# A graph layer's second stage, regrouped: attribute turns once in eight rows, accumulator banks cleared by ScalarE, two rows mixed in one product, one-hots built per row

## The reference

```
h   = segment_sum(x[dst] * weight, src) @ W.T            # layer 1
x1  = layernorm(x + h)
# layer 2: tensor product of the 9 edge attributes with the source node
msg = sum_m attr[e, m] * (x1[src[e]] @ M_m)              # M_m: 128 x 128, built from w0..w4
y   = segment_sum(msg, dst)
out = layernorm(x1 + y)
```

## Time and profile before

| | |
|---|---|
| time, median of 3 runs | 4115.09 us (4114.18 to 4115.81) |
| the profiled execution's own time: its span | 5011.3 us |
| instructions recorded | 63448 |
| first gather of the second layer | at 1859.7 us |
| last gather of the second layer | at 4968.6 us |

### The profile page before, as it was taken

One profiled execution on the slowest core, in us unless ns is written; L12 is line 12 of the kernel. 1 busy time (PEld: TensorE's weight loads), 2 busy tenths in 40 slices (PEclk: granted clock), 3 DMA queues, 4 the chain that ended last, 5 costly groups with the idle time before them and its releaser, 6 DMA issues.

```text
span 5011.3 us, 63448 instructions
## 1 busy us (share of the span) xinstructions
PE 3029.2 (60%) x18004; PEld 2599.8 (52%) x18006; DVE 2089.5 (42%) x4613; ACT 1176.6 (23%) x2104; POOL 2759.7 (55%) x2887
## 2 busy tenths in 40 slices
PE   2100788888888864555555555555556555555666
PEld 1000778788887863444444444444445444444555
DVE  8999565565565661222222222222222222222333
ACT  5443444444444440000000000000000000000111
POOL 4000555555555536666666666666666666666664
PEclk6555899999999976777777777777777777777666
DMA  1001222222222231111111111111111111111221
GB/s 49 5 11 41 75 71 75 71 71 76 72 71 71 71 96 47 46 47 46 46 46 46 46 47 46 46 46 46 46 47 47 46 47 45 46 46 55 66 66 46
DMA packets 117978, 267.07 MB, mean 53 GB/s; under 512 B 52225, under 2 KB 52369, under 8 KB 116769
## 3 DMA queue, kind: packets, MB, share of 16 engines
q0 software_dynamic: 92080, 191.02, 13.1%
q1 hardware_dynamic: 21234, 66.99, 3.9%
q10 hardware_dynamic: 4608, 8.39, 0.4%
HBM read 251.19 MB, written 8.72 MB: 52 GB/s over the span
## 4 chain that ended last, share of the span: by engine, by line
another core or an unknown queue 34%; PE 11%; issue 10%; DVE 6%; DVEq 2%; ACT 0%; ACTq 0%
PE quad L1673 5%; PE mixed L1688 4%; DVE group L1784 3%; DVE hot L1758 1%; PE quad L1666 1%; PE attr_t L1639 1%; DVE acc L1790 1%; DVEq L1769 1%; DVE attr_hot L1763 0%; DVEq L1784 0%; DVEq L1758 0%; DVEq L1777 0%; DVEq L1780 0%; DVEq L1761 0%
## 5 line engine op out<-in xcount | busy, mean ns | idle before, releaser
L1558 POOL DMA_INDIRECT feat<-x,ids x2048 | 1940.6, 948 | 1181.8 <-issue 615.8
L1784 DVE TENSOR_TENSOR group<-group,quad 128x504 f32 (+1 forms) x512 | 347.3, 678 | 2301.9 <-remote 2167.5
L1134 POOL DMA_INDIRECT l_feat<-in_x,id_of x768 | 737.4, 960 | 916.5 <-ACT w_of L827 368.7
L1673 PE MATMUL quad<-attr_hot,feat 128*128 128x144 f32 x4096 | 842.8, 338 | 547.7 <-issue 544.3
L1673 PEld LDWEIGHTS quad<-attr_hot,feat 128*128 128x128 f32 x4096 | 661.0, 219 | 737.5 <-issue 736.4
L1688 PE MATMUL mixed<-group,mix 128*128 128x192 f32 x2304 | 691.1, 486 | 577.9 <-DVE group L1784 577.9
L1688 PEld LDWEIGHTS mixed<-group,mix 128*128 128x128 f32 x2304 | 650.5, 305 | 622.7 <-issue 556.8
L1599 ACT CAST ids<-src_col 128x8 int32 (+1 forms) x256 | 50.3, 197 | 2746.0 <-remote 2525.4
L1208 PE MATMUL got<-x_near,far_w 128*128 128x128 bf16 x4224 | 341.0, 220 | 160.3 <-issue 148.6
L1208 PEld LDWEIGHTS got<-x_near,far_w 128*128 128x128 bf16 x4224 | 278.7, 98 | 206.4 <-issue 192.1
L1036 DVE TENSOR_SCALAR keys<-swap,src_of,w_of 128x184 f32<-128x184 f32 x1024 | 308.2, 373 | 127.9 <-PE l_pre L1227 122.0
(11 more groups left out here) (249 smaller groups left out, 2929.8 us busy)
## 6 DMA issues: line engine op xcount, KB each, us to landing
place<-table SPq DMA_DIRECT2D x64, 640.0 KB
feat<-x,ids POOLq DMA_INDIRECT x2048
l_feat<-in_x,id_of POOLq DMA_INDIRECT x768
attr_in<-in_edge_attr SPq DMA_DIRECT2D x129, 72.0 KB
norm_x<-in_x SPq DMA_DIRECT2D x16, 256.0 KB, 2.7
x<-norm_z ACTq DMA_DIRECT2D x16, 256.0 KB, 2.4
x_t<-x SPq DMA_DIRECT2D x15, 256.0 KB
out<-z_t ACTq DMA_DIRECT2D x15, 256.0 KB
```

Of the source, the lines that this page charges most:

```text
L1134: pool.indirect_dma_start(feat[:, landing, :], None, x, bass.IndirectOffsetOnAxis(ap=id_of[s % 2][:, c:c + 1], axis=0)).then_inc(feat_in[l ...
L1558: pool.indirect_dma_start(feat[z][:, t, :], None, x1, bass.IndirectOffsetOnAxis(ap=ids[z][h][:, t % H:t % H + 1], axis=0),).then_inc(feat_ ...
L1673: last = nc.tensor.matmul(bank[:, :, bass.ds(places[t % H], WIN)], feat[z][:, t, :], attr_hot[h][:, t % H, :, :], start=False, stop=(t % Q ...
L1784: nc.vector.tensor_tensor(to, to, quad[:, q, 0:NA * QUAD_WIN].rearrange("p (m n) -> p m n", m=NA), ALU.add).then_inc(quad_added, 1)
```

## The change

The second layer is regrouped around steps of eight rows (an octet):

- attributes of eight rows are loaded at once (576 KB, 128 partitions) and turned by nine 128x128 transposes, in two parts, in the third and fifth row of each octet; ScalarE copies them from `attr_t` into the SBUF tile `attr_e`, from which VectorE reads;
- ScalarE clears the banks of `quad`, two at a time, after VectorE has added them; the matmuls by zeros go;
- two rows share one `group` tile and are mixed by one set of nine matmuls of 384 columns, one row later; VectorE adds both halves after that;
- `hot` and `attr_hot` are made once for each row, two rows ahead; `ids` once for four rows;
- POOL's loop has eight rows; its gathers and their waits on `half_summed` stay; they count on one semaphore per half row instead of one per quad.

```diff
-        ids = [[sb(f"ids{z}_{h}", [P, H], I32) for h in range(2)] for z in range(ROW_SLOTS)]
-        attr_in = [sb(f"attr_in{z}", [R, P * NA], F32) for z in range(2)]
-        hot = sb("hot", [P, H, WIN], F32)
-        attr_hot = [sb(f"attr_hot{h}", [P, H, NA, WIN], F32) for h in range(2)]
-        group = [sb(f"group{z}", [P, NA, GROUP_WIN], F32) for z in range(2)]
+        ids = [sb(f"ids{b}", [P, O // 2 * R], I32) for b in range(2)]
+        attr_in = sb("attr_in", [O * R, P * NA], F32)
+        attr_e = sb("attr_e", [P, NA, O * R], F32)
+        hot = sb("hot", [P, R, WIN], F32)
+        attr_hot = [sb(f"attr_hot{z}", [P, R, NA, WIN], F32) for z in range(2)]
+        group = [sb(f"group{z}", [P, NA, 2, GROUP_WIN], F32) for z in range(2)]
...
# GpSimd
+                with pool.Fori(0, OCTETS) as o:
+                    for j in range(O):
+                        z = j % S
+                        if j % (O // 2) == 0:
+                            pool.wait_ge(ids_made, w * (2 * OCTETS) + o * 2 + (j // (O // 2) + 1))
                         for h in range(2):
-                            pool.wait_ge(ids_made, w * (RN * 2) + i * (2 * ROW_SLOTS) + (z * 2 + h + 1))
+                            pool.wait_ge(half_summed, summed(w, o * O, (j - S) * 2 + h))
                             pool.sem_inc(g.turn, 1)
...
# ScalarE
+                def row(o, j, first=False, e=None):
+                    r = o * O + j
+                    u = w * RN + r
+                    if j % 2 == 1 and not (first and j == 1):
+                        act.wait_ge(pair_mixed, w * PAIRS + o * (O // 2) + (j - 3) // 2 + 1)
+                        clear_group((j - 3) // 2)
+                    act.wait_ge(quad_added, u * 4 + 2)
+                    clear_half(0)
+                    if e is not None:
+                        normalize(w, e)
+                    act.wait_ge(quad_added, u * 4 + 4)
+                    clear_half(1)
+                    if j % (O // 2) == O // 2 - 1:
+                        act.wait_ge(half_summed, summed(w, r, 1))
+                        copy_ids(...)
+                    if j == TURN_ROW - 1:
+                        copy_last()
+                    if j == TURN_ROW + 1:
+                        copy_attr(w * OCTETS + o + 1)
...
# TensorE
+                pe.wait_ge(quad_zero, u * 2 + (h + 1))
+                if h == 0:
+                    pe.wait_ge(hot_made, u + 2)
+                pe.wait_ge(feat_in[z % S][h], n_fill * (16 * H) + 16 * H)
+                for t in range(h * H, h * H + H):
+                    (the matmul of L1673, attr_hot[z % 2][:, t, :, :])
...
+                def row(o, j, first=False):
+                    for h in range(2):
+                        half_row(w, r, h, j, n_fill)
+                    if j % 2 == 0 and not (first and j == 0):
+                        mix(w * PAIRS + o * (O // 2) + (j - 2) // 2, (j - 2) // 2 % 2)
+                    turn_next(w * OCTETS + o + 1, j)
...
# VectorE
-                by_tile = attr_t[:, z, 0:NA * R].rearrange("p (m t) -> p t m", m=NA)
-                nc.vector.tensor_tensor(attr_hot[h][:], hot[:].unsqueeze(2).to_broadcast(s4),
-                                        by_tile[:, h * H:h * H + H, :].unsqueeze(3).to_broadcast(s4),
-                                        ALU.mult).then_inc(hot_made, 1)
+                by_tile = attr_e[:, :, j * R:(j + 1) * R].rearrange("p m t -> p t m")
+                nc.vector.tensor_tensor(attr_hot[z][:], hot[:].unsqueeze(2).to_broadcast(s4),
+                                        by_tile.unsqueeze(3).to_broadcast(s4), ALU.mult).then_inc(hot_made, 1)
...
+                    add_quads(w, r, n, j // 2 % 2, j % 2, 0, offs)
+                    if starts:
+                        add_pair(n - 1, starts)
+                    add_quads(w, r, n, j // 2 % 2, j % 2, 1, offs)
+                    next_hots(o, j)
```

More of the change, by code:

```diff
@@ L1543, in _ @@
             n_loads = sp.value_load(g.n_pass[0:1, 1:2], min_val=1, max_val=g.PASSES1)
-            for z in range(2):
-                sp.wait_ge(attr_here[z], n_loads * (8 * RN) + 16 * (1 - z))
+            sp.wait_ge(attr_here, n_loads * (16 * OCTETS) + 32)
             sp.sem_inc(loads_ended, 1)
@@ L1588, in _ @@
                 act.sem_inc(stored[s], 16)
[L1589 to L1592, removed]
-            with passes(act) as w:
[L1594 to L1606, removed]
+            for b in range(2):
+                copy_ids(b, b * (O // 2 * R))
@@ new lines, in mix @@
+            def mix(n, side):
+                pe.wait_ge(quad_added, n * 8 + 8)
+                pe.wait_ge(acc_added, n * 2 + 2)
+                pe.sem_inc(g.turn, 1)
+                to = mixed[:, 0:2 * GROUP_WIN].rearrange("p (a n) -> p a n", a=2)
+                for m in range(NA):
+                    last = nc.tensor.matmul(to, g.mix[:, m, :], group[side][:, m, :, :], start=(m == 0),
+                                            stop=(m == NA - 1))
+                last.then_inc(pair_mixed, 1)
@@ new lines, in turn_nodes @@
+            def turn_nodes(w, u, e):
+                pe.wait_ge(acc_added, u + 2 - e % 2)
+                pe.wait_ge(x_used, w * NE + e + 2)
+                pe.sem_inc(g.turn, 1)
+                for a in range(BATCH):
+                    last = nc.tensor.transpose(y[:, a * P:(a + 1) * P], nodes_of(e)[:, a, :],
+                                               g.cst[:, C_IDENT:C_IDENT + P])
+                last.then_inc(y_made, 1)
+            pe.wait_ge(attr_here, 16)
+            turn_attr((NA - 1,))
@@ L1658, in _ @@
+            pe.wait_ge(attr_out, 1)
+            turn_attr(range(NA - 1))
+            pe.wait_ge(tables_made, 1)
             with passes(pe) as w:
-                def row(r, half_r, z, v_half, e=None):
-                    u = w * RN + r
-                    turn_attr(u + 1, v_half, 1 - z)
+                def row(o, j, first=False):
+                    r = o * O + j
+                    n_fill = o * (O // S) + j // S
                     for h in range(2):
[L1663 to L1676, removed]
-                        if h == 0 and e is not None:
-                            pe.wait_ge(acc_added, u + 2)
-                            pe.wait_ge(x_used, w * NE + e + 2)
-                            pe.sem_inc(g.turn, 1)
-                            for a in range(BATCH):
-                                last = nc.tensor.transpose(y[:, a * P:(a + 1) * P], nodes_of(e)[:, a, :],
-                                                           g.cst[:, C_IDENT:C_IDENT + P])
-                            last.then_inc(y_made, 1)
-                    pe.wait_ge(quad_added, u * 4 + 8)
-                    pe.wait_ge(acc_added, u + 2)
-                    for m in range(NA):
-                        last = nc.tensor.matmul(mixed[:, 0:GROUP_WIN], g.mix[:, m, :], group[z][:, m, :],
-                                                start=(m == 0), stop=(m == NA - 1))
-                    return last
@@ L1697, in _ @@
-                for r in range(EARLY, RN):
-                    last_mixed = row(r, r // 2, r % 2, w * (RN // 2) + (r // 2 + r % 2), batch_of(r))
-                last_mixed.then_inc(half_summed, 1)
+                for j in range(O):
+                    row(0, j, first=True)
+                with pe.Fori(1, LOOPED) as o:
+                    for j in range(O):
+                        row(o, j)
+                mix(w * PAIRS + (EARLY // 2 - 1), (EARLY // 2 - 1) % 2)
+                for r in range(EARLY, RN):
+                    half_row(w, r, 0, r, r // S)
+                    if batch_of(r) is not None:
+                        turn_nodes(w, w * RN + r, batch_of(r))
+                    half_row(w, r, 1, r, r // S)
+                    if r % 2 == 1:
+                        mix(w * PAIRS + r // 2, r // 2 % 2)
+                    turn_next(w * OCTETS + (r // O + 1), r % O)
@@ L1833, in _, with next_hots @@
-                dve.wait_ge(first_turned, 1)
-                hots(w * RN, 0, 0, 0, pass_begun(w))
-                hots(w * RN, 0, 1, 0, pass_begun(w))
-                row(0, 0, first=True)
-                row(0, 1)
-                with dve.Fori(1, EARLY // 2) as i:
-                    row(i, 0)
-                    row(i, 1)
-                for r in range(EARLY, RN):
-                    row(r // 2, r % 2, last=(r == RN - 1))
+                def next_hots(o, j):
+                    if (j + 2) % O == 0:
+                        dve.wait_ge(attr_out, w * (2 * OCTETS) + o * 2 + 4)
+                    r = o * O + (j + 2)
+                    hots(w * RN + r, r, (j + 2) % O, j % 2)
@@ new lines, in row @@
+                def row(o, j, first=False):
+                    r = o * O + j
+                    n = w * PAIRS + o * (O // 2) + j // 2
+                    if j % 2 == 0 or first and j == 1:
+                        starts, offs = [], load_places(r * Q + 1, Q - 1)
+                    else:
```

(16 more changed lines are left out.)

236 lines of the change are left out of this document (141 added, 95 removed).

## The result

The time after is 4325.64 us, median of four runs (4324.70 to 4328.93), against 4115.45 us for the kernel before in the same comparison (4114.18 to 4116.51). The ratio is 1.0511 [1.0496, 1.0526]: 210 us slower.

What follows compares the result with a forecast made beforehand. POOL was taken to bound the timed runs at x = 18.5 us a row. After less before, 128x + 230 + 27 - (112x + 336) = 217 us, on 4115 gives 4332, say 4330 us; range 4075 to 4435.

Steps and rivals of the forecast that it cites:

- the likeliest case: Second layer: POOL-bound and the attr_hot product holds POOL; 4330 us, own range 4230 to 4435, chance 0.70.
- rival (1): Second layer: POOL sets the pace and the attr_hot product holds its gathers; 4330 us, chance 0.70.
- Rival (3): Second layer: TensorE's chain of 17.1 us a row limits timed runs, the change shortens it; 4076 us, chance 0.12.
- rival (4): Second layer: TensorE's chain limits timed runs, the change shortens it, and the product holds nothing; 3833 us, chance 0.04.
- Rival (5): Second layer: the new order makes a chain longer than POOL's 16 gathers; above 4330 us, chance 0.02.
- x: POOL's time for the 16 gathers of a second-layer row in timed runs: 18.5 us, from 17.1 to 19.8.
- 16x - 309: What the last 16 rows were said to give back, before's taken at 19.8 us each: between nothing and 36 us.
- The removed work costs nothing, the added work beside POOL costs nothing: Looped rows: dropped zero matmuls, narrow transposes and mix wait save nothing; new ScalarE, SP and TensorE work stays hidden.
- The product holds POOL: attr_hot, one 2.55 us product a row with both factors in SBUF, delays a gather by 1.8 us, from 1.17 to 2.42.
- Rival (2): Second layer: POOL-bound, but the product, its factors being broadcast views, doesn't hold it; 4102 us, chance 0.12.
- The tail: From the end of the changed kernel's last gather to the end: 27 us, with 9 for the double mix.
- the stretch of TensorE: TensorE's matmuls spread out while POOL issues in the first trace; taken as belonging to the recording, absent from timed runs.

Runs made afterwards that it cites:

- before profiled again: The kernel before, unchanged, timed and profiled a second time: 4115.24 us.
- the halved gathers: Before, after, and after with one product factor in PSUM in 112 rows, each gathering only every second tile and using it twice: 3373.30, 3098.75 and 2878.61 us.
- the changed before: The kernel before with ScalarE copying the turned attributes from PSUM to SBUF, so both factors of VectorE's two products a row lie there: 4232.67 us.

## Why the prediction was right

The prediction was 4330 us, the time 4325.6, inside the likeliest case's own range. The mechanism of rival (1) held. Two of its terms were off, by 23 us one way and 18 the other; that they nearly cancel, and that the number is so close, is luck.

- **POOL sets the pace of the timed runs.** Shown, by before profiled again, where no gather waited, and by the halved gathers: before's chain without POOL is 13.66 us a row at the clock given above, where I had read 13.8 off the last row. Rival (3) falls with it, and rival (4). Rival (5) falls with the rows of 20.01 us in the regrouped kernel.
- **x was mis-sized.** I took 18.5, at most 19.8; it is 20.0, the traced step. The step that failed is "if all that stands ahead of 1859.7 us costs the same in a timed run". It began 331 us earlier. The sentence behind it had the bound: if the first layer is shorter too, x goes to 20.0. The effect on the sum: 16x - 309 is 11 by my formula and 5 as measured (the difference of the tails), not -13. This term was there since I took the last 16 rows of before as chain-bound at 19.8 us; they ran at POOL's 20.0 like all others, so they give nothing back. The sentence on it has the sign reversed as well: what they give back is 309 - 16x. And the upper end of the range comes to 4433 by its own terms, not 4435.
- **The removed work costs nothing, the added work beside POOL costs nothing.** Shown: with the factor in PSUM the first 112 rows take 20.01 us, as before's do, with all the rest of the change in them.
- **The product holds POOL.** Shown three ways: take the SBUF factor away and the loss goes; give it to before and it comes; double it and it grows, while twice the product with a PSUM factor costs nothing. Rival (2) falls. The product's duration was 2.559 us for 2.55. The price of one hold, what is left less 0.12 or 0.13, fits all 128 gathers of after that start more than 0.04 us into a product. The mean was mis-sized: 1.62 us a row (207 over 128 rows), not 1.8. I had taken all phases as equally likely. They aren't: in two rows of three the loss is 1.3 us, in the third 2.2 (the middle rows above show one of each). Of the 127 rows behind the first, 114 have one long gather and 12 have two.
- **The tail** was 24.5 us and not 27, since the double mix took 6.0 us and not 9, and 5 longer than before's. The sum with measured terms is 207 + 5 = 212 us, for 210 measured. Mine was 230 - 13 = 217.
- **The span** was forecast at 4680 us for a profiled execution like the first. The one I got was 4323.8, so the stretch of TensorE under it was neither shown nor refuted; its cause stays open. The one row that the forecast shares, 21.8 us, stands against a mean of 21.6.

The Trainium skill (SBUF — State Buffer, section Who interferes with whom) says that a tensor_tensor with both inputs in SBUF contends with GpSimd's reads. The trace agrees: 2.26 us lost behind 2.39 of a product. The same section reports that tensor_tensor didn't stall a DMA; for the indirect transfers here, whose indices lie in SBUF (`ids`), the measurement differs.

## What to carry to other kernels

Where POOL issues indirect transfers back to back and sets the pace, price a VectorE product by where its inputs lie: with two SBUF inputs it holds each gather that starts in its time, with one in PSUM it holds none, at the same duration. That is shown for this product and not for every VectorE step (two of another kind, with one SBUF tile as input, hold gathers too, see below). A copy from PSUM to SBUF ahead of a product can therefore cost more than all that the regrouping around it saves. And when span and timed runs differ, don't place the excess in the stage under study: take what holds without it (here a step of 1.25 us) as the first value.

## What was not expected of the hardware

- The hold depends on who starts first. A gather that starts before a product isn't held, however little before: those at 3033.54 in after (0.94 us; product at 3033.66) and at 3012.04 in the changed before (0.94; product at 3012.06). Nor is one that starts up to 0.044 us behind it; there the product itself is 0.03 to 0.07 us longer. From 0.046 us on every gather is held to the product's end, less 0.11 to 0.13 us: over 700 of them in the traces of products with two SBUF factors. So the hold falls on something near a gather's start, most likely its reading of the indices; that was not tried by itself.
- Two SBUF tiles as inputs aren't the only case. The first gathers of the layer also start in two steps that read one tile and a single column, in before profiled again:

```profile
1531.16 1.03 DVE L1739 TENSOR_SCALAR tile_offs<-off_f,keep 128x1536 int32<-128x1536 f32 x1
1531.72 1.29 POOL L1558 DMA_INDIRECT feat<-x,ids  x1 [0.31 <-issue]
...
1533.78 1.52 DVE L1743 TENSOR_SCALAR off_f<-tile_start,keep 128x2048 f32<-128x2048 f32 x1
1534.57 1.55 POOL L1558 DMA_INDIRECT feat<-x,ids  x1 [0.31 <-issue]
```

They meet 0.47 and 0.73 us and lose 0.34 and 0.60: the same price. The first of the two already stood in the earlier trace rows. No run here varies these steps.

- The same kernel's profiled execution was 5011.3 us once and 4113.5 us once. The two differ in the first layer as well (1859.7 and 1529.2 us), while a POOL record's median was 947 ns in both the earlier trace rows.
- TensorE's matmuls into the quads take 409 ns each in after and 353 in before profiled again, same shape, same count. The timeline of after shows two speeds:

```profile
3017.44 4.18 PE L1727 MATMUL quad<-attr_hot,feat 128*128 128x144 f32 x16 [8.42 <-DMA feat<-x,ids]
...
3038.74 2.20 PE L1727 MATMUL quad<-attr_hot,feat 128*128 128x144 f32 x16
```

The granted clock is 0.50 from 3017.5 to 3021.5 us, after 8.42 us without work, and 1.00 from 3038.7 to 3040.9, behind a mix and transposes: 1.2 and 2.4 GHz. The regrouped kernel's TensorE has less to do and longer pauses (busy for 56% of the span, before 69%), and a mean granted clock of 0.71 for 0.73 in the rows. TensorE waits for the gathers in both, so it costs nothing here.
